# Strassen's seven products for gate and up in blocks 2 to 7, with weight sums kept in DRAM and streamed

## The chip, the cores and the metric

The kernel runs on one core of one Trainium2 chip. The metric is the device time of one execution in microseconds (us), as the median of several runs. Engines are named as in the profile: PE is TensorE's matmul, PEld its weight load, DVE is VectorE, ACT is ScalarE, POOL is GpSimd, SP is the engine that issues most DMAs.

## The reference, cut to what matters

Input x is 4 x 1024 tokens of 512 numbers in float32. Both branches start from one layer norm.

```python
xn = _layernorm(x)
# attention branch (16 heads of 32, chunks of 128 tokens, decaying state S per head)
h = _rmsnorm(xn, qkv_norm_w);  q, k, v = split(h @ _weight_quant(qkv_w).T)
scores = einsum('bhtd,bhsd,hts->bhts', q, k, mask)
o = scale * (scores @ v + (q * lam_t) @ S);  S = lam_T * S + (k * lam_rev).T @ v
attn = _rmsnorm(_rmsnorm(o, norm_w), proj_norm_w) @ _weight_quant(proj_w).T
# feed-forward branch, hidden width 2048
gate = xn @ w_gate.T;  up = xn @ w_up.T
ffn = (silu(gate) * up) @ w_down.T
return x + attn + ffn
```

## The kernel before

The 4096 tokens are cut into 8 blocks of 512. A block is 4 chunks of 128 tokens. Float32 operands are split into a high and a low float16 part, and a product is made of three matmuls (high x high, high x low, low x high); the quantized weights of the attention branch need one part, so theirs is made of two. `products` (line 517 is its matmul) issues them.

Each block is a list of items, and each engine has its own list, written out by hand: `FIRST_ORDER` for block 0, which also prepares the weights, and `STEADY_ORDER` for blocks 1 to 7. An engine runs its items strictly in that order and waits on semaphores that the other engines raise. The items are:

- `K`, `Q` (8 each, 256 tokens wide) and `V` (4, 512 columns): projections. ACT and DVE split the results (`K` and `Q` at L661 and L748), and SP copies them by DMA into `k_stack` and `q_stack` (three DMAs each, L935 and L937).
- `SC` (16): scores of four heads, L559. DVE multiplies by the mask (`SC`, L789), ACT and DVE split (`SC` at L673, `SL` at L747). `O` (L586, L588) and `OX` are the attention products, `KV` the update of the state.
- `G` and `U` for each of 16 tiles of 128 hidden columns: gate and up products, 12 matmuls of 512 columns each. ACT takes SiLU of the gate (L728), DVE multiplies by the up product (`U`, L908), ACT and DVE split the result (`UH` at L735, `UL` at L747).
- `D` (16): down products, 12 matmuls of 512 columns each, added to `y` by DVE (L861). `PJ` (4, 8 matmuls each): the output projection.
- `NA`, `NR`, `NZ`, `ZT`: the norms of the attention output and its transposes by DMA (L1019). `KT` is a transpose of K (L1015).
- `ST`, `XN`, `TX`, `TH`: statistics and norm of the next block's x, its split, and its transposes by DMA into `xt` (four of 1024 columns, L1007 and L1012) and `ht` (L999). The `xt` ones wait until all `G` and `U` of the block have run, since `xt` has one buffer. `YS` stores the output.

All gate and up weights stay in SBUF (`wg`, `wu`). PSUM has 8 banks: gate, up, scores, attention output, and four shared by the other products in turn.

## Time and profile before

| | |
|---|---|
| median of 3 runs | 1361.49 us (1361.11 to 1363.04) |
| the profiled execution's own time | 1361.45 us |
| its span | 1359.7 us |
| granted TensorE clock | 1.00 |
| PE busy | 1334.2 us (98%), 8332 matmuls |
| DVE busy | 924.6 us (68%) |
| ACT busy | 486.5 us (36%) |
| POOL busy | 67.5 us (5%) |
| DMA | 98.72 MB, mean 73 GB/s |

Busy times are unions of the instructions' spans. Spans of consecutive matmuls overlap, so the pace of a stream of matmuls is read from the starts of its first and next instructions, not from the mean duration. Block 1 runs from about 184.5 to 342.2 us and a steady block takes 164.6 us (671.7 to 836.3 is one).

### The profile page before, as it was taken

How to read it: one execution, taken by the hardware profiler on the slowest of the kernel's cores; microseconds unless marked ns; L12 is line 12 of the kernel's file. 1: busy time of each engine (PE TensorE's matmuls, PEld its weight loads, DVE VectorE, ACT ScalarE, POOL GpSimd, SP SyncE). 2: the span in 40 equal slices, each digit the busy share in tenths (PEclk: the TensorE clock that was granted, in tenths of full speed). 3: DMA queues.
4: the chain of work that ended last, by engine and by line, in shares of the span. 5: the costliest groups of instructions: out<-in, count | busy, mean ns of one | idle time of the engine just before them, and what ended most of it. 6: DMA issues, size and time to landing. Idle time of an engine off the chain costs nothing.

```text
span 1359.7 us, 21928 instructions
## 1 busy us (share of the span) xinstructions
PE 1334.2 (98%) x8332; PEld 721.3 (53%) x8332; DVE 924.6 (68%) x1886; ACT 486.5 (36%) x915; POOL 67.5 (5%) x88
## 2 busy tenths in 40 slices
PE   5899999999999999999999999999999999999999
PEld 3455555555455554555545555555545555455554
DVE  6988995576655766657766677657775576755655
ACT  7964633233233332333323233223332233232331
POOL 5600000000000000000000000000000000000000
DMA  8242234113431145211351113510145112431121
GB/s 314 83 142 67 87 73 120 26 32 67 111 88 28 30 79 124 53 32 40 71 140 35 29 40 70 148 40 26 38 85 132 32 30 49 94 94 32 32 48 47
DMA packets 193767, 98.72 MB, mean 73 GB/s; under 512 B 127104, under 2 KB 179328, under 8 KB 192000
## 3 DMA queue, kind: packets, MB, share of 16 engines
q1 hardware_dynamic: 193376, 97.30, 28.3%
q8 instruction: 68, 1.11, 0.4%
q14 instruction: 35, 0.29, 0.1%
q10 hardware_dynamic: 288, 0.01, 0.0%
HBM read 34.35 MB, written 8.39 MB: 31 GB/s over the span
## 4 chain that ended last, share of the span: by engine, by line
PE 94%; DVE 3%; ACT 1%; DMA 1%; SPq 1%; issue 1%; POOL 0%; DVEq 0%; POOLq 0%
PE bank L517 89%; PE bank L559 2%; PE bank L586 1%; PE bank L588 1%; DVE wg_lo L1292 0%; SPq L935 0%; DMA xin<-x 0%; ACT wg_lo L1142 0%; DMA k_stack<-k_parts 0%; DVE arena L861 0%; DMA q_stack<-q_parts 0%; DVE arena L747 0%; DVE xt L748 0%; DVE wd_lo L1292 0%; DVE wu_lo L1292 0%
## 5 line engine op out<-in xcount | busy, mean ns | idle before, releaser
L517 PE MATMUL bank<-wd_hi,arena 128*128 128x512 f16 x1024 | 317.0, 379 | 0.0
L517 PE MATMUL bank<-xt,wg_hi 128*128 128x512 f16 x1024 | 306.5, 381 | 3.6 <-ACT ql L728 1.6
L517 PE MATMUL bank<-xt,wu_hi 128*128 128x512 f16 x1024 | 304.6, 379 | 0.0
L517 PE MATMUL bank<-xt,wg_lo 128*128 128x512 f16 x512 | 195.0, 381 | 0.0
L517 PE MATMUL bank<-wd_lo,arena 128*128 128x512 f16 x512 | 194.0, 379 | 0.0
L517 PE MATMUL bank<-xt,wu_lo 128*128 128x512 f16 x512 | 194.0, 379 | 0.0
L517 PEld LDWEIGHTS bank<-wd_hi,arena 128*128 128x128 f16 x1024 | 100.2, 98 | 115.3
L789 DVE TENSOR_TENSOR sm<-bank,mask 128x512 f32<-128x512 f32 x128 | 88.1, 688 | 105.4 <-PE bank L559 105.3
L517 PEld LDWEIGHTS bank<-xt,wu_hi 128*128 128x128 f16 x1024 | 99.0, 98 | 104.4 <-issue 0.5
L517 PEld LDWEIGHTS bank<-xt,wg_hi 128*128 128x128 f16 x1024 | 98.2, 98 | 103.5 <-issue 4.6
L673 ACT ACTIVATE sm_hi<-sm 128x512 f16<-128x512 f32 x128 | 80.1, 626 | 193.5 <-DVE sm L789 193.5
L908 DVE SCALAR_TENSOR_TENSOR sg<-bank,small,sg 128x512 f32<-128x512 f32 x125 | 93.4, 747 | 76.7 <-ACT sg L728 41.4
L861 DVE SCALAR_TENSOR_TENSOR arena<-bank,small,arena 128x512 f32<-128x512 f32 x160 | 119.6, 748 | 36.0 <-PE bank L517 33.5
L728 ACT ACTIVATE sg<-bank,small 128x512 f32<-128x512 f32 x125 | 85.6, 685 | 130.1 <-PE bank L517 79.5
L517 PE MATMUL bank<-ht,wq 128*128 128x256 f16 x1024 | 124.8, 273 | 0.8 <-issue 0.8
L747 DVE TENSOR_TENSOR sm_lo<-sm,sm_hi 128x512 f16<-128x512 f32 x128 | 88.1, 688 | 52.4 <-ACT sm_hi L673 52.3
L517 PEld LDWEIGHTS bank<-ht,wq 128*128 128x128 f16 x1024 | 97.3, 98 | 14.6 <-issue 1.3
L747 DVE TENSOR_TENSOR arena<-sg,arena 128x512 f16<-128x512 f32 x125 | 85.6, 684 | 9.7 <-ACT arena L735 9.1
L735 ACT ACTIVATE arena<-sg 128x512 f16<-128x512 f32 x125 | 77.7, 622 | 34.6 <-DVE sg L908 34.4
L517 PEld LDWEIGHTS bank<-xt,wg_lo 128*128 128x128 f16 x512 | 50.2, 98 | 61.1 <-issue 1.1
L517 PEld LDWEIGHTS bank<-xt,wu_lo 128*128 128x128 f16 x512 | 50.0, 98 | 60.5
L661 ACT ACTIVATE k_parts<-bank 128x256 f16<-128x256 f32 x64 | 24.4, 382 | 155.5 <-PE bank L517 155.5
(200 smaller groups left out, 1492.2 us busy)
## 6 DMA issues: line engine op xcount, KB each, us to landing
k_stack<-k_parts SPq DMA_DIRECT2D x192, 64.0 KB, 2.2
q_stack<-q_parts SPq DMA_DIRECT2D x192, 64.0 KB, 2.2
arena<-x SPq DMA_DIRECT2D x8, 1024.0 KB, 5.9
out<-arena SPq DMA_DIRECT2D x32, 256.0 KB, 2.4
xin<-x SPq DMA_DIRECT2D x30, 256.0 KB, 4.5
stage<-up_t SPq DMA_DIRECT2D x4, 1024.0 KB, 5.3
stage<-down_t SPq DMA_DIRECT2D x4, 1024.0 KB, 4.9
stage<-gate_t SPq DMA_DIRECT2D x3, 1024.0 KB, 4.8
```

The source lines that it names most:

```text
L517: last = e.matmul(dst, a, b, start=start and n == 0, stop=stop and n == len(lhs) - 1)
L559: last = e.matmul(b_sc[:, P * h:P * (h + 1)], k_stack[:, h, t], q_stack[:, h, t], start=True, stop=True)
L586: e.matmul(both[:, h, :, :], smp[0][:, h, :], vh, start=h == 0, stop=False)
L588: last = e.matmul(both[:, h, 0, :], smp[1][:, h, :], vh[:, 0, :], start=False, stop=alone)
L661: e.activation(parts[:, 0, :], bank_of(it, blk)[:, 0:HALF], ACT.Copy, scale=QKV_SCALE).then_inc(ac[kind].sem, 1)
L673: e.activation(smp[0][:, :, :], sm[:, :, :], ACT.Copy).then_inc(ac["SM"].sem, 1)
L728: e.activation(gate_tile(blk, h), b_gate[:, :], ACT.Silu, scale=sgate[:, q:q + 1]).then_inc(ac["SILU"].sem, 1)
L735: e.activation(gated[q % 2][0][:, h % HPQ, :], gate_tile(blk, h), ACT.Copy).then_inc(ac["GH"].sem, 1)
L747: return e.tensor_tensor(dst, src, hi, ALU.subtract)
L789: e.tensor_tensor(sm[:, :, :], b_sc[:, :].rearrange("p (h t) -> p h t", h=HPG), mask[:, HPG * j:HPG * (j + 1), :], ALU.mult).then_inc(ve[" ...
L861: e.scalar_tensor_tensor(out=y[:, c, :], in0=bank_of(it, blk)[:, :], scalar=beta[:, 8:9] if kind == "PJ" else cd[:, it[1]:it[1] + 1], in1= ...
L908: e.scalar_tensor_tensor(out=gate_tile(blk, h), in0=b_up[:, :], scalar=cu[:, q:q + 1], in1=gate_tile(blk, h), op0=ALU.mult, op1=ALU.mult). ...
```

## The change

Blocks 0 and 1 keep the plain gate and up products (`PLAIN = 2`). Blocks 2 to 7 use the Winograd form of Strassen's scheme. For a tile, the gate and the up weights are the two rows of a 2 x 2 block matrix whose columns are the two halves of the 512 input features; x has the two halves of the features by two halves of the block's tokens. Seven products of such blocks take the place of eight. Each is a unit of six matmuls of 256 columns (2 slices of the contraction, 3 combinations of parts).

- **PE**: `G` and `U` give way to `TA` (two units), `TB` (three), `TC` (one), `TD` (one) for each tile.
- **ACT** copies partial sums out of PSUM at `TA`, `TB` and `TC` (s1, s2, s3, 256 columns each); its `TD` is SiLU on the finished gate tile. **DVE** adds them to other banks: `TA` (C11, 256 columns), `TC` (C2, 512), `TD` (C12, 256). **POOL** multiplies SiLU's result by the up tile (`UG`). `UH` and `UL` split that with the scale `cu`; `UL` becomes a scaled form.
- **x**: `TX` gives way to `XC`: POOL makes four sums of 256 columns per pair of chunks (`TT`), ACT and DVE split seven units of 256 columns, and SP transposes 3584 columns by one DMA, twice a block (`move_c`), into `xs`, which has one buffer.
- **Weights**: the sums of weights are made in block 1, one tile at a time in two slots: `BL` (two loads), `BS` (scale, ACT), `BA` (four sums, POOL), `BH` and `BC` (high and low parts of 1792 columns, ACT and DVE), `BX` (store of 128 x 3584 float16 to a DRAM tensor). From block 2 on `LW` on ACT's queue loads tile after tile into a ring of four buffers.
- Block 1 has an order of its own (`SECOND_ORDER`); `STEADY_ORDER` is written anew. The plain weights and the new buffers share one SBUF tensor, `wide`. Two shared banks are left in blocks 2 to 7. Scales by powers of two change (`X_SCALE` and others).

The diff, cut to its core:

```diff
--- before.py
+++ after.py
+UNITS = 7
+UNIT = KT * P // 2
+RING = 4
+PLAIN = 2
 SMALL = 267
...
-X_SCALE = 2.0 ** 10
+X_SCALE = 2.0 ** 9
 H_SCALE = 2.0 ** 9
+W_SCALE = 2.0 ** 12
+GATED_SCALE = 2.0 ** 5
...
+BUILD_SLOT = [0 if h < 2 else h % 2 for h in range(HT)]
...
 STEADY_ORDER = {
     "PE": [
-        ('K', 0), ('Q', 0), ('U', 0), ('V', 0), ('G', 0), ('V', 1), ('SC', 0, 0), ('G', 1), ('U', 1), ('KV', 0), ('O', 0, 0),
...
+        ('K', 0), ('V', 0), ('V', 1), ('Q', 0), ('TA', 0), ('TA', 1), ('TB', 0), ('TC', 0), ('TB', 1), ('TD', 0), ('TC', 1),
+        ('TA', 2), ('SC', 0, 0), ('TD', 1), ('TB', 2), ('TC', 2), ('O', 0, 0), ('SC', 0, 1), ('KV', 0), ('K', 1), ('TA', 3),
+        ('Q', 1), ('TD', 2), ('TB', 3), ('TC', 3), ('TA', 4), ('OX', 0, 0), ('O', 0, 1), ('SC', 1, 0), ('TD', 3),
...
+        ('D', 2, 3), ('D', 3, 0), ('D', 3, 1), ('PJ', 1), ('D', 3, 2), ('D', 3, 3), ('PJ', 2), ('PJ', 3),
...
-    wg = [sb(f"wg_{n}", [P, KT, HID], F16) for n in ("hi", "lo")]
-    wu = [sb(f"wu_{n}", [P, KT, HID], F16) for n in ("hi", "lo")]
+    wide = sb("wide", [P, NQ, 4 * KT * HID // NQ], F16)
...
+    b_work = [wide[:, n, 0:both].bitcast(F32) for n in range(2)]
+    b_out = [wide[:, n, both:2 * both] for n in range(2)]
+    f32_part = lambda start, n: wide[:, 0, 2 * start:2 * (start + n)].bitcast(F32)
+    gt = [f32_part(BLK * n, BLK) for n in range(3)]
+    up = [f32_part(BLK * (3 + n), BLK) for n in range(2)]
+    s1, s3 = (f32_part(5 * BLK + HALF * n, HALF) for n in range(2))
+    s2 = [f32_part(6 * BLK + HALF * n, HALF) for n in range(2)]
+    xs = wide[:, 1, 0:2 * both].rearrange("p (a t) -> p a t", t=HALF)
+    ring = [wide[:, 2 + n // 2, both * (n % 2):both * (n % 2 + 1)] for n in range(RING)]
+    comb = [wide[:, 2, 2 * both:2 * both + 2 * D].bitcast(F32), osq]
...
+        elif kind in ("TA", "TB", "TC", "TD"):
+            h = it[1]
+            one, two = b_tile[h % 2]
+            low, high = slice(0, HALF), slice(HALF, 2 * HALF)
+            def unit(dst, w, b, start=True):
+                for k in range(2):
+                    for n in range(3):
+                        last = e.matmul(dst, tile_weights(h, n // 2, w, k), tile_x(n % 2, b, k),
+                                        start=start and (k, n) == (0, 0), stop=(k, n) == (1, 2), skip_group_check=not start)
...
+            if kind == "TA":
...
+                e.wait_ge(ld_w[h % RING].sem, ld_w[h % RING].at(blk, 16 * (h // RING + 1)))
+                e.wait_ge(ve["C12"].sem, ve["C12"].at(blk, h - 1))
+                unit(one[:, low], 0, 0).then_inc(pe["P1"].sem, 1)
+                unit(two[:, low], 1, 1).then_inc(pe["P2"].sem, 1)
+            elif kind == "TB":
+                e.wait_ge(ac["S1"].sem, ac["S1"].at(blk, h + 1))
+                unit(one[:, low], 4, 4, start=False).then_inc(pe["P6"].sem, 1)
+                e.wait_ge(ve["C11"].sem, ve["C11"].at(blk, h + 1))
+                unit(two[:, low], 3, 6)
+                unit(two[:, high], 2, 3)
+            elif kind == "TC":
+                e.wait_ge(ac["S2"].sem, ac["S2"].at(blk, h + 1))
+                unit(one[:, low], 5, 5, start=False).then_inc(pe["P7"].sem, 1)
+            else:
+                e.wait_ge(ve["C2"].sem, ve["C2"].at(blk, h + 1))
+                unit(two[:, high], 6, 2, start=False).then_inc(pe["P3"].sem, 1)
         elif kind == "D":
             _, q, c = it
...
+        elif kind == "XC":
+            p = it[1]
...
+            dst = c_src[p]
+            e.wait_ge(moved_c[p].sem, moved_c[p].at(blk, 0))
+            e.activation(dst[:, 0:D], xin[:, 0, :], ACT.Copy).then_inc(ac["XC"].sem, 1)
+            e.activation(dst[:, D:D + UNIT], xin[:, 1, UNIT:D], ACT.Copy).then_inc(ac["XC"].sem, 1)
+            e.wait_ge(po["TT"].sem, po["TT"].at(blk, p + 1))
+            for n in range(2):
+                a = 3 * UNIT + D * n
+                e.activation(dst[:, a:a + D], comb[n], ACT.Copy).then_inc(ac["XC"].sem, 1)
+        elif kind == "TA":
+            h = it[1]
+            e.wait_ge(pe["P1"].sem, pe["P1"].at(blk, h + 1))
+            e.wait_ge(ve["C11"].sem, ve["C11"].at(blk, h))
+            e.activation(s1, b_tile[h % 2][0][:, 0:HALF], ACT.Copy).then_inc(ac["S1"].sem, 1)
+        elif kind == "TB":
+            h = it[1]
+            e.wait_ge(pe["P6"].sem, pe["P6"].at(blk, h + 1))
+            e.wait_ge(ve["C12"].sem, ve["C12"].at(blk, h - 1))
+            e.activation(s2[h % 2], b_tile[h % 2][0][:, 0:HALF], ACT.Copy).then_inc(ac["S2"].sem, 1)
+        elif kind == "TC":
+            h = it[1]
+            e.wait_ge(pe["P7"].sem, pe["P7"].at(blk, h + 1))
+            e.wait_ge(ve["C2"].sem, ve["C2"].at(blk, h))
+            e.activation(s3, b_tile[h % 2][0][:, 0:HALF], ACT.Copy).then_inc(ac["S3"].sem, 1)
+        elif kind == "TD":
+            h = it[1]
+            q, t = h // HPQ, gt[h % 3]
+            e.wait_ge(ve["C12"].sem, ve["C12"].at(blk, h + 1))
+            e.activation(t, t, ACT.Silu, scale=sgate[:, q:q + 1]).then_inc(ac["SILU"].sem, 1)
+        elif kind == "LW":
+            h = it[1]
+            if is_plain(blk):
+                e.wait_ge(st_b[BUILD_SLOT[h - HT]], 16 * turn(h - HT))
+                e.wait_ge(pe["U"].sem, pe["U"].at(blk, 12 if h < HT + 2 else HT))
+            else:
+                e.wait_ge(pe["P3"].sem, pe["P3"].at(blk, h - RING + 1))
+            e.dma_start(ring[h % RING], made[h % HT, :, :]).then_inc(ld_w[h % RING].sem, 16)
         elif kind == "G":
...
+        elif kind == "XC":
+            for n, (a, src) in enumerate(((0, xin[:, 0, :]), (D, xin[:, 1, UNIT:D]), (3 * UNIT, comb[0]), (5 * UNIT, comb[1]))):
+                size = UNIT if n == 1 else D
+                last = lo(dst[:, UNITS * UNIT + a:UNITS * UNIT + a + size], src, 1.0, dst[:, a:a + size], ac["XC"], 4 * p + n + 1)
+            last.then_inc(ve["XC"].sem, 1)
...
+        elif kind == "TA":
+            h = it[1]
+            e.wait_ge(ac["S1"].sem, ac["S1"].at(blk, h + 1))
+            e.wait_ge(pe["P2"].sem, pe["P2"].at(blk, h + 1))
+            e.wait_ge(po["GT"].sem, po["GT"].at(blk, max(h - 2, 0)))
+            e.tensor_tensor(gt[h % 3][:, 0:HALF], b_tile[h % 2][1][:, 0:HALF], s1, ALU.add).then_inc(ve["C11"].sem, 1)
+        elif kind == "TC":
+            h = it[1]
+            e.wait_ge(ac["S3"].sem, ac["S3"].at(blk, h + 1))
+            e.wait_ge(ve["GL"].sem, ve["GL"].at(blk, max(h - 1, 0)))
+            e.tensor_tensor(up[h % 2].rearrange("p (a t) -> p a t", a=2),
+                            b_tile[h % 2][1][:, :].rearrange("p (a t) -> p a t", a=2),
+                            s3.unsqueeze(1).to_broadcast([P, 2, HALF]), ALU.add).then_inc(ve["C2"].sem, 1)
+        elif kind == "TD":
+            h = it[1]
+            e.wait_ge(pe["P3"].sem, pe["P3"].at(blk, h + 1))
+            e.tensor_tensor(gt[h % 3][:, HALF:2 * HALF], b_tile[h % 2][1][:, HALF:2 * HALF], s2[h % 2], ALU.add)\
+                .then_inc(ve["C12"].sem, 1)
         elif kind == "U":
             h = it[1]
             q = h // HPQ
...
+        if it[0] == "UG":
+            h = it[1]
+            e.wait_ge(ac["SILU"].sem, ac["SILU"].at(blk, h + 1))
+            e.tensor_tensor(up[h % 2], up[h % 2], gt[h % 3], ALU.mult).then_inc(po["GT"].sem, 1)
+        elif it[0] == "TT":
+            p = it[1]
+            a, b, (t1, t2), (t3, t4) = xin[:, 0, :], xin[:, 1, :], *([t[:, 0:UNIT], t[:, UNIT:D]] for t in comb)
+            e.wait_ge(ve["XN"].sem, ve["XN"].at(blk, 2 * p + 2))
+            if is_plain(blk):
+                e.wait_ge(pe["U"].sem, pe["U"].at(blk, 3 * HPQ))
+            e.tensor_tensor(t3, b[:, UNIT:D], b[:, 0:UNIT], ALU.subtract).then_inc(po["T3"].sem, 1)
+            e.tensor_tensor(t1, b[:, 0:UNIT], a[:, 0:UNIT], ALU.subtract)
+            e.wait_ge(po["T3"].sem, po["T3"].at(blk, p + 1))
+            e.tensor_tensor(t2, t3, a[:, 0:UNIT], ALU.add).then_inc(po["T2"].sem, 1)
...
+                def move_c(p):
+                    if not is_plain(blk):
+                        e.wait_ge(pe["P3"].sem, pe["P3"].at(blk, HT))
+                    e.wait_ge(ve["XC"].sem, ve["XC"].at(blk, p + 1))
+                    e.dma_start_transpose(xs[:, :, P * p:P * (p + 1)], c_src[p]).then_inc(moved_c[p].sem, 16)
...
+                    elif kind == "BX":
+                        e.wait_ge(s_built, n + 1)
+                        e.dma_start(made[n, :, :], b_out[BUILD_SLOT[n]]).then_inc(st_b[BUILD_SLOT[n]], 16)
+                    elif kind == "BL":
+                        m, (q, i) = BUILD_SLOT[n], divmod(n, HPQ)
+                        e.wait_ge(pe["U"].sem, pe["U"].at(blk, HPQ * (m + 1)))
+                        if turn(n) > 1:
+                            e.wait_ge(s_built, max(g + 1 for g in range(n) if BUILD_SLOT[g] == m))
+                        for u, which in enumerate(("gate", "up")):
+                            e.dma_start(b_work[m][:, D * u:D * (u + 1)].rearrange("p (k c) -> p k c", k=KT),
+                                        dram[which][q, :, :, P * i:P * (i + 1)]).then_inc(ld_b[m], 16)
...
+                elif kind == "BA":
+                    a11, a12, s1_, a22, s2_, s3_, s4_ = (b_work[BUILD_SLOT[n]][:, UNIT * u:UNIT * (u + 1)] for u in range(UNITS))
+                    e.wait_ge(s_bscaled, n + 1)
+                    e.tensor_tensor(s3_, a11, s1_, ALU.subtract).then_inc(s_blink, 1)
+                    e.wait_ge(s_blink, 3 * n + 1)
+                    e.tensor_tensor(s1_, s1_, a22, ALU.add).then_inc(s_blink, 1)
+                    e.wait_ge(s_blink, 3 * n + 2)
+                    e.tensor_tensor(s2_, s1_, a11, ALU.subtract).then_inc(s_blink, 1)
+                    e.wait_ge(s_blink, 3 * n + 3)
...
+                elif kind == "BS":
+                    m = BUILD_SLOT[n]
+                    e.wait_ge(ld_b[m], 32 * turn(n))
+                    for u, which in enumerate(("gate", "up")):
+                        w, at = b_work[m][:, D * u:D * (u + 1)], PIECES.index((which, n // HPQ))
+                        last = e.activation(w, w, ACT.Copy, scale=ws[:, at:at + 1])
+                    last.then_inc(s_bscaled, 1)
+                elif kind == "BH":
+                    m = BUILD_SLOT[n]
+                    e.wait_ge(s_badd, n + 1)
+                    if turn(n) > 1:
+                        e.wait_ge(st_b[m], 16 * (turn(n) - 1))
...
+                elif kind == "BC":
+                    m = BUILD_SLOT[n]
+                    e.wait_ge(s_bhi, n + 1)
+                    e.tensor_tensor(b_out[m][:, UNITS * UNIT:both], b_work[m], b_out[m][:, 0:UNITS * UNIT], ALU.subtract)\
+                        .then_inc(s_built, 1)
...
```

## Rows read from the trace of the kernel before

**Rows 1.** The page: busy us, share of the span, instructions.

```profile
PE 1334.2 (98%) x8332; PEld 721.3 (53%) x8332; DVE 924.6 (68%) x1886; ACT 486.5 (36%) x915; POOL 67.5 (5%) x88
```

**Rows 2.** PE's waits: us in total, times, longest.

```profile
PE bank L1168 <- ACT wg_lo L1142: 12.6, 2, 12.1
PE bank L517 <- ACT ql L728: 1.6, 1, 1.6
```

**Rows 3.** Windows: length; PE, PEld, DVE, ACT, POOL busy; clock, DMA share, GB/s.

```profile
671.70:836.30 164.60, 164.60 (x1034) 88.46 (x1032) 109.33 (x222) 52.03 (x104) 3.81 (x4) 1.00 0.27 65
...
184.50:342.20 157.70, 156.37 (x985) 85.06 (x984) 104.81 (x213) 50.65 (x102) 3.91 (x4) 1.00 0.29 67
```

**Rows 4.** PE's timeline: start us, us, instruction.

```profile
707.85 0.60 PE L517 MATMUL bank<-xt,wg_hi 128*128 128x512 f16 x2
...
710.44 0.59 PE L517 MATMUL bank<-xt,wu_hi 128*128 128x512 f16 x2
...
713.80 1.91 PE L517 MATMUL bank<-ht,wq 128*128 128x256 f16 x16
715.55 0.59 PE L517 MATMUL bank<-xt,wg_hi 128*128 128x512 f16 x2
```

**Rows 5.** Groups by form: busy us, mean ns | idle before.

```profile
L908 DVE SCALAR_TENSOR_TENSOR sg<-bank,small,sg 128x512 f32<-128x512 f32 x125 | 93.4, 747 | 76.7 <-ACT sg L728 41.4 <-PE bank L517 35.0
...
L728 ACT ACTIVATE sg<-bank,small 128x512 f32<-128x512 f32 x125 | 85.6, 685 | 130.1 <-PE bank L517 79.5 <-DVE arena L747 50.6
L747 DVE TENSOR_TENSOR arena<-sg,arena 128x512 f16<-128x512 f32 x125 | 85.6, 684 | 9.7 <-ACT arena L735 9.1
...
L822 DVE TENSOR_TENSOR arena<-bank,arena 128x256 f32<-128x256 f32 x64 | 27.1, 423 | 45.5 <-ACT arena L686 45.1
...
L686 ACT ACTIVATE arena<-bank 128x256 f32<-128x256 f32 x64 | 24.5, 382 | 66.2 <-PE bank L517 66.2
...
L1292 DVE SCALAR_TENSOR_TENSOR wd_lo<-stage,small,wd_hi 128x1024 f16<-128x1024 f32 x8 | 9.9, 1278 | 0.0
...
L1136 ACT ACTIVATE wd_hi<-stage,small 128x1024 f16<-128x1024 f32 x8 | 8.9, 1146 | 0.0
```

**Rows 6.** Timeline of POOL, then of DVE, block 0.

```profile
44.05 1.98 POOL L1084 TENSOR_SCALAR wu_lo<-wu_lo,small 128x1024 f32<-128x1024 f32 x1
46.12 1.04 POOL L1085 TENSOR_SCALAR wu_lo<-wu_lo 128x1024 f32<-128x1024 f32 x1
...
57.85 0.62 POOL L1090 TENSOR_SCALAR lam_q<-lam_q 128x512 f32<-128x512 f32 x1
...
44.96 0.68 DVE L747 TENSOR_TENSOR ht<-bank,ht 128x512 f16<-128x512 f32 x1
...
46.22 2.02 DVE L1292 SCALAR_TENSOR_TENSOR wu_lo<-stage,small,wu_hi 128x1024 f16<-128x1024 f32 x1
```

**Rows 7.** DMA issues: count, KB each, median us to landing.

```profile
q_stack<-q_parts SPq DMA_DIRECT2D x192, 64.0 KB, 2.2
...
out<-arena SPq DMA_DIRECT2D x32, 256.0 KB, 2.4
...
stage<-gate_t SPq DMA_DIRECT2D x3, 1024.0 KB, 4.8
...
xt<-stage SPq DMA_TRANSPOSE x28, 3.1
```

**Rows 8.** Timeline of SP, then of PE, around step 1.

```profile
718.49 0.60 SPq L937 DMA_DIRECT2D q_stack<-q_parts  x1
...
720.95 0.38 PE L559 MATMUL bank<-q_stack,k_stack 96*128 96x128 f16 x4
```

**Rows 9.** Timeline at a block's end: PE, SP, PE.

```profile
671.68 0.19 PE L586 MATMUL bank<-v,sm_hi 128*128 128x64 f16 x1
...
687.55 3.44 SPq L1012 DMA_TRANSPOSE xt<-stage  x2
...
698.99 0.59 PE L517 MATMUL bank<-xt,wu_hi 128*128 128x512 f16 x2
```

294 lines of the change are left out of this document (203 added, 91 removed), and 152 rows, old and new, of tables (SECOND_ORDER, STEADY_ORDER, ve).

## The prediction

> **What bounds the kernel now.** The page's busy table comes first: TensorE (PE) is busy for 1334.2 us, 98% of the span [rows 1]. A busy share alone does not say who waits, so the list of PE's waits comes next. Its largest entry is 12.6 us in the opening, and the next is 1.6 us [rows 2]. Then the windows: in one steady block, 671.7 to 836.3 us, PE is busy for all 164.60 us, DVE for 109.33, ACT for 52.03, the DMA share is 0.27, and the granted clock is 1.00. Block 1 (184.5 to 342.2) shows 156.37 of 157.70 [rows 3]. So PE's stream of matmuls sets the end, and whatever leaves that stream is a gain, as long as nobody new makes PE wait. Every engine runs a hand-written order in sequence, so one late result stops all that stands behind it.
>
> **The matmuls removed (blocks 2 to 7).** The timeline gives the pace, since durations overlap. A gate product G is 12 matmuls of 512 columns, from 707.85 to 710.44 us: 2.59 us, 216 ns each. A K and a Q product are 16 matmuls of 256 columns, from 713.80 to 715.55: 1.75 us, 109.4 ns each [rows 4]. A tile's G and U cost 24 x 216 ns = 5.18 us. The new tile is 7 units x 6 = 42 matmuls of 256 columns, 42 x 109.4 = 4.59 us. The weight loads double in rate, but K and Q already run at one load per 256 columns, so 109.4 ns holds it. Saved: 0.585 us x 16 tiles x 6 blocks = 56 us. Blocks 0 and 1 issue the same matmuls as before. This is also the most the change can give: 1361.45 - 56 = 1305.
>
> **Work added to ACT and DVE (steady).** From [rows 5]: DVE loses U (0.75) and gets TA 0.42, TC 0.69 (512 columns) and TD 0.42 per tile; UL goes from 0.68 to the scaled form, 0.75. That is +0.85 us x 16 = 14 us. XC computes 2 x 1792 columns of low parts where TX computed 4 x 512, +2 us. DVE comes to 109 + 16 = 125 of a block of 164.6 - 9.4 = 155.2 us: 81%. ACT gets three copies of 256 columns, 3 x 0.38 x 16 = 18 us, some 2 us in XC and 20 DMA issues, about 80 of 155. Neither is a bound on its sum. Hidden under PE they cost nothing; if one stood on the path, its excess would be paid in full. Inside a tile the waits are short and covered: TB's first unit waits for a copy (0.38) made while the other tile's TA (1.3 us) runs, TC's result (S3, then C2: 0.38 + 0.69) has TA or TB of the next tile (1.3 to 2.0 us) before TD needs it. SiLU's product moves to POOL (UG), and UL stands behind it in DVE's order. Two shared banks instead of four: a product waits until the one before last is emptied. At the tightest place, V(1) behind K(0), that takes 0.38 + 2 x 0.42 us under V(0)'s 8 x 216 ns = 1.73 us; 0.5 us of slack, charged at nothing. The changed powers of two cost no instruction.
>
> **POOL beside DVE.** No row shows a two-input product of 512 columns on POOL. Nearest rows: one input of 512 columns took 0.62 us; one input of 1024, which reads as much as two of 512, took 1.04 at 46.12 and 1.98 at 44.05 [rows 6]. I take 1.1 us inside 0.62 to 2.0. What contention does is in the same group. DVE's 1024-column operation at 46.22 reads two SBUF operands and took 2.02 us, just behind POOL's start at 46.12 (its usual mean is 1.28 [rows 5]). The one at 44.96 reads PSUM and took 0.68 us beside POOL, no more than elsewhere. In a steady block DVE will have 88 instructions with two SBUF operands (16 SL, 16 UL, 16 state sums, 8 KT, 8 head products, 8 in XC, four each of NA, NZ, ZT and H), some 50 us. POOL will be busy 16 x 1.1 + 8 x 0.6 = 22 us of 155, 14%. 88 x 0.14 x half of 1.1 = 7 us more on DVE, 132 in all, 85%. Still under PE, so I charge nothing. The lower bound of this term is 0; the upper, each of the 88 waiting 0.55 us, is 48 us, and DVE would then take 173 us a block, above the old PE time.
> The Trainium skill (SBUF — State Buffer, on the shared port pair) says that a DVE instruction with two SBUF inputs and a GpSimd instruction that reads SBUF exclude each other, the later fully blocked. The slowed and the undisturbed row above agree with it, and it speaks against this change. By the rule at its worst the sum would be rival D's; by the rows' overlap it stays as it is.
>
> **The weight stream.** Each tile's sums are 128 x 3584 f16, 0.9 MB, 16 of them a block. A 1024 KB load lands after 4.8 us and a 256 KB transfer after 2.4 [rows 7], so 768 KB cost 2.4 us and a tile 2.8: 45 us a block, over the 44 us of 0.27 x 164.6. With 3072 more columns to transpose (4 us, priced below) the share is about 0.6, no bound. The ring of four keeps loads some three tiles (25 us) ahead. The price is delay for the small copies. The last copy of Q(1) into its stack is issued at 718.49 us and takes 2.2 us [rows 7]; the score product runs at 720.95 [rows 8]: 0.25 us of slack. The new order leaves 4.9 us between Q(1) and SC(1,0), and sends K 1.3 us earlier, so SP is free: 0.6 (ACT) + 1.3 (issue) + 2.2 = 4.1, 0.6 to 0.8 us of slack. A step meets a weight load with chance 45/155 = 0.3 and is held 1.4 us on average. 8 steps x 0.3 x (1.4 - 0.6) = 1.9 us a block, 11 us in all (0 if the loads always fall between; 8 x 1.4 x 6 = 67 if they always collide).
>
> **The block's end (steady).** Before, the last attention product starts at 671.68, the last x transpose is the second of the two issued in the 3.44 us from 687.55, so issued about 689.8 and landed 3.1 us later, 692.9, and U(0) reads it at 698.99 [rows 7, 9]: slack 6 us on a chain of 21. After, the chain gets POOL's four sums (4 x 0.6 = 2.4 us), 0.5 us of longer copies, and a transpose of 3584 columns in place of 1024. Of the 3.1 us for 1024 columns the part that grows with size is between 0.9 (a 64 KB copy's 2.2 us taken off) and 3.1; I take 1.4, near the lower end, so 2560 columns more are 3.5 us (2.3 to 7.8). ZT moved behind XN gives back 1.3. Chain: 26.1 us. Cover from O(7,1) to TA(0), with V(0) and V(1) now ahead: TD .66, six D 15.5, three PJ 5.2, K, V, V, Q 5.2 = 26.6. Slack 0.5 us, and the load LW 18 issued just before it takes up to 2.8 us of the same queues. I charge 1 us x 5 = 5 (0 to 4 each, so up to 20).
>
> **Block 1, where the sums are made.** 16 times: two loads, BS (2 x 0.69), four POOL sums (2.6), BH (1792 columns, from 1.15 for 1024: 1.7), BC (from 1.28 and 0.68: 2.2), a store [rows 5]. With the load, 3 to 5 us, a slot turns in 10.8 to 12.9 us before any queueing. From D(0,0) to D(2,3) PE has 16 G and U, 11 D and small work, 81 us, for six turns: 13.5 us each. DVE is at 105 + 34 = 139 of 158. Nearly no room for three in-order queues, and POOL's 64 sums meet DVE's. I charge 8 us, between 0 and 3 us x 7 turns + 4 = 25. What is late then is BX(15), st_b, both transposes and TA(0) of block 2.
>
> **Sum.** 1361.45 (this execution's time; the median of the runs is 1361.49) - 56 + 11 + 5 + 8 = 1329.5, say 1330.
>
> **Rivals.**
> A. Everything is hidden: 1305 to 1315. For: before, PE waited for nothing in steady blocks although a chain had 0.25 us of slack. Against: DVE goes from 66% to 85%. Chance 0.2.
> B. The forecast, 1315 to 1345: chance 0.55.
> C. The block's end and block 1 cost their upper bounds, 20 and 25 us, with 11 us inside the blocks: 1361.45 - 56 + 56 would be no gain at all, and part of that gives 1345 to 1358. For: the 0.5 us of slack; a store and two long transposes behind the last sum. Chance 0.13.
> D. The other side: POOL and DVE exclude each other at nearly each of the 88 instructions. PE waits at all once DVE's blocked time passes 155 - 125 = 30 us a block, and the gain is gone at 39.4 us; at 48 us the block takes 173 us, 6 x 8.4 = 50 us slower, 1412. For: the rows at 44 to 47 us. Against: POOL's 22 us leave little to block. Chance 0.07.
> E. C in full, or C with part of D, so that nothing or less than nothing is left, 1358 to 1370: chance 0.05.
>
> Faster by more than 0.2% (2.7 us, about what a measurement of this kernel can tell from no change): A, B and C, 0.88; within it 0.03 and slower 0.09, from D and E. The range from 1307 to 1352 holds most of A, all of B and two thirds of C, 0.81.
>
> **What would show it.** In the windows of a steady block: length 157 to 160 us, PE idle 2 to 5 us. 256-column matmuls at 109 ns, 42 a tile; if they pace at 115 or more, the 56 us is wrong. In PE's waits: rows released by stack copies, by xs transposes at each TA(0), and in block 1 by the sums. DVE busy near 130 us, POOL's product near 1.1 us; if POOL shows 2 us or PE waits mostly for DVE's C2 and C12, D was at work. A block 1 longer than 185 us would make the time longer than the range allows.

## The result and the profile after

The changed kernel takes 1538.93 us (median of four runs, 1534.20 to 1550.50); the kernel before took 1362.26 beside it (1361.11 to 1364.17). The ratio is 1.131, with a 95% interval of 1.124 to 1.138: 13% slower, where 1330 us was forecast. The profiled execution took 1534.20 us, its span is 1532.4.

From the page after: busy time, then PE's granted clock and the DMA share in 40 slices (compare [rows 1]).

```profile
PE 1339.8 (87%) x10060; PEld 903.7 (59%) x10060; DVE 1088.7 (71%) x2118; ACT 648.5 (42%) x1275; POOL 294.3 (19%) x296
...
PEclk9999999999889999999999999899998999989999
DMA  7232342477955349553594435944468543595342
```

PE's busy time is about what it was, but it is now 87% of the span: PE is idle for 193 us where it was idle for 25. PE's waits name the places (as in [rows 2]). Columns: us in total, times, longest. L811 is the first unit of a Strassen tile, L721 the score product.

```profile
PE bank L811 <- issue: 38.1, 6, 9.2
PE bank L721 <- issue: 34.3, 10, 6.2
PE bank L721 <- DMA k_stack<-k_parts: 25.6, 20, 3.3
PE bank L721 <- DMA q_stack<-q_parts: 22.1, 8, 4.0
PE bank L679 <- DVE arena L1109: 21.7, 17, 4.4
```

82 us stand ahead of score products, which wait for their stacked operands; 38 stand ahead of the first tile of a block, six times, once in each block that follows the building or a Strassen block. Windows of block 1 and of the first two Strassen blocks (columns as in [rows 3]), cut at SP's issue of the load of x into y, which comes once a block:

```profile
212.30:422.90 210.60, 178.69 (x1047) 92.88 (x1048) 151.79 (x241) 99.83 (x157) 72.49 (x76) 0.94 0.64 181
422.90:613.40 190.50, 167.05 (x1339) 120.69 (x1337) 131.24 (x258) 71.87 (x157) 30.91 (x28) 0.96 0.57 137
613.40:799.40 186.00, 165.37 (x1333) 120.31 (x1331) 129.55 (x255) 71.98 (x158) 30.72 (x28) 0.96 0.58 141
```

DVE's 131 us and the DMA share of 0.57 are as forecast (132 and 0.6). What is new is the length, 186 to 190 us against 155 us of matmuls, and a clock of 0.96. Cut at the same issue, the blocks of the kernel before are 164 to 166 us long, block 1 among them.

One such wait from near, in block 2: four lines of SP and ACT (what they issue), then three of PE.

```profile
438.12 1.25 SPq L1234 DMA_DIRECT2D q_stack<-q_parts  x2
439.41 0.60 SPq L1236 DMA_DIRECT2D q_stack<-q_parts  x1
...
438.37 0.33 ACTq L966 DMA_DIRECT2D wide<-made  x1
...
440.99 0.33 ACTq L966 DMA_DIRECT2D wide<-made  x1
```

```profile
448.05 0.59 PE L721 MATMUL bank<-q_stack,k_stack 96*128 96x128 f16 x4 [6.24 <-issue]
448.43 1.48 PE L811 MATMUL bank<-wide 128*128 128x256 f16 x6
449.71 0.63 PE L679 MATMUL bank<-state,ql 128*128 128x128 f32 x2
```

ACT issues two weight loads, one 0.25 us after SP's first copy and one 1.6 us after its last. The last copy is issued at 439.41, and a copy usually takes 2.2 us; PE starts only at 448.05, 8.6 us later, after 6.24 us of idleness. The view of q_stack has 8.6 us as its longest landing, so this is the copy that PE waited for, though the profile shows the wait as "issue". The windows over this stretch show what follows (granted clock and DMA share are the two numbers before the last):

```profile
440.00:444.00 4.00, 1.81 (x23) 1.55 (x21) 1.33 (x3) 0.81 (x3) 1.27 (x1) 1.00 1.46 285
444.00:448.00 4.00, 0.00 (x0) 0.00 (x0) 0.00 (x0) 0.00 (x0) 0.00 (x0) 0.82 0.51 166
448.00:452.00 4.00, 3.95 (x21) 3.04 (x22) 1.02 (x2) 0.72 (x3) 0.00 (x0) 0.50 0.20 61
```

PE stood still from 441.8 to 448.0 and then worked at a granted clock of 0.50, the lower of its two levels (1.2 of 2.4 GHz): six matmuls of 256 columns take 1.28 us from start to start (448.43 to 449.71), 213 ns each, against 109 at the full clock. So a wait is paid a second time. In "PE busy" this shows as work, which is why PE is as busy as before with 56 us less of it to do.

The block's end. SP's two long transposes of the sums of x, at the end of block 1, and PE's first tile of block 2:

```profile
392.41 4.21 SPq L1288 DMA_TRANSPOSE wide<-stage  x1
399.35 13.01 SPq L1288 DMA_TRANSPOSE wide<-xt  x1
```

```profile
416.67 1.65 PE L811 MATMUL bank<-wide 128*128 128x256 f16 x7 [8.11 <-issue]
```

The DMA issues (count, KB, median us to landing; transposes without KB) and, below them, the last line of the view of k_stack:

```profile
wide<-made ACTq DMA_DIRECT2D x96, 896.0 KB, 5.6
...
out<-arena SPq DMA_DIRECT2D x32, 256.0 KB, 10.4
```

```profile
wide<-stage SPq DMA_TRANSPOSE x6, 6.4
wide<-xt SPq DMA_TRANSPOSE x6, 17.0
...
DMA to landing us min/median/max: 2.1/2.2/9.4
```

A copy still lands after 2.2 us in the median; only some are late, by up to 7 us. Copies are not alone in this: the transposes into `stage`, K's among them, land after up to 11.9 us (9.1 before). The second transpose takes 17 us in the median, the first, of the same size, 6.4.

### The profile page after: what moved, and what is told of

The parts are those of the page before. It is cut to its first block, busy times and chain, and to the rows that moved or that the text cites. A ratio compares the mean times of both kernels' runs of the same rounds, so it can differ in the third digit from the quotient of the medians.

```text
span 1532.4 us, 26734 instructions
## 1 busy us (share of the span) xinstructions
PE 1339.8 (87%) x10060; PEld 903.7 (59%) x10060; DVE 1088.7 (71%) x2118; ACT 648.5 (42%) x1275; POOL 294.3 (19%) x296
## 4 chain that ended last, share of the span: by engine, by line
PE 55%; DVE 18%; issue 9%; DMA 8%; SPq 5%; ACT 3%; POOL 2%; ACTq 0%; DVEq 0%; POOLq 0%
PE bank L679 30%; PE bank L811 22%; DMA k_stack<-k_parts 4%; SPq L1234 3%; DVE stage L995 2%; DMA q_stack<-q_parts 2%; PE bank L721 2%; DVE arena L1109 2%; DVE wide L1661 1%; DMA wide<-up_t 1%; SPq L1335 1%; DVE sm_lo L995 1%; DVE xin L1132 1%; DVE sm L1037 1%; SPq L1236 1%
## 5 line engine op out<-in xcount | busy, mean ns | idle before, releaser
L811 PE MATMUL bank<-wide 128*128 128x256 f16 x4032 | 498.2, 281 | 38.3 <-issue 38.1
L811 PEld LDWEIGHTS bank<-wide 128*128 128x128 f16 x4032 | 402.8, 101 | 100.6 <-issue 40.9
L1204 POOL TENSOR_TENSOR wide<-wide 128x512 f32<-128x512 f32 x96 | 125.9, 1314 | 823.8 <-ACT wide L958 823.8
L679 PE MATMUL bank<-xt,wide 128*128 128x512 f16 x768 | 178.1, 387 | 6.7 <-ACT sg L972 3.3
L679 PEld LDWEIGHTS bank<-xt,wide 128*128 128x128 f16 x768 | 75.1, 100 | 94.7 <-issue 9.9
L721 PE MATMUL bank<-q_stack,k_stack 96*128 96x128 f16 x512 | 50.9, 223 | 82.1 <-issue 34.3
L1174 DVE TENSOR_TENSOR wide<-bank,wide 128x512 f32<-128x512 f32 x96 | 66.1, 689 | 50.4 <-ACT wide L953 48.8
L1169 DVE TENSOR_TENSOR wide<-bank,wide 128x256 f32<-128x256 f32 x96 | 40.2, 419 | 63.9 <-ACT wide L943 47.7
L1180 DVE TENSOR_TENSOR wide<-bank,wide 128x256 f32<-128x256 f32 x96 | 40.3, 419 | 63.5 <-PE bank L811 62.7
L721 PEld LDWEIGHTS bank<-q_stack,k_stack 96*128 96x128 f16 x512 | 31.9, 98 | 88.7 <-issue 88.3
L679 PEld LDWEIGHTS bank<-wd_lo,arena 128*128 128x128 f16 x512 | 50.8, 99 | 52.4 <-issue 3.1
L996 DVE SCALAR_TENSOR_TENSOR arena<-wide,small,arena 128x512 f16<-128x512 f32 x96 | 80.6, 840 | 0.4
```

The lines of the kernel that those rows point to most:

```text
L679: last = e.matmul(dst, a, b, start=start and n == 0, stop=stop and n == len(lhs) - 1)
L721: last = e.matmul(b_sc[:, P * h:P * (h + 1)], k_stack[:, h, t], q_stack[:, h, t], start=True, stop=True)
L811: last = e.matmul(dst, tile_weights(h, n // 2, w, k), tile_x(n % 2, b, k), start=start and (k, n) == (0, 0), stop=(k, n) == (1, 2), skip_g ...
L996: return e.scalar_tensor_tensor(out=dst, in0=src, scalar=scale, in1=hi, op0=ALU.mult, op1=ALU.subtract)
L1174: e.tensor_tensor(up[h % 2].rearrange("p (a t) -> p a t", a=2), b_tile[h % 2][1][:, :].rearrange("p (a t) -> p a t", a=2), s3.unsqueeze(1) ...
L1180: e.tensor_tensor(gt[h % 3][:, HALF:2 * HALF], b_tile[h % 2][1][:, HALF:2 * HALF], s2[h % 2], ALU.add)\
```

## The experiments

Unless said otherwise each ran once, beside the kernel before, which took 1361.3 to 1363.7 us (the median where it ran several times). The changed kernel's own runs differ by 16 us from each other, so smaller steps from it are not read. The kernel with all loads issued by SP took 1401.6 us in one series and 1407.2 to 1409.3 in another; from it, steps under 8 us are not read. Lengths of blocks 1 to 6, cut as above:

| kernel | us | block 1 | blocks 2 to 6 |
|---|---|---|---|
| before | 1361.5 | 164.3 | 164.3, 165.8, 163.6, 165.5, 164.1 |
| changed | 1534.2 | 210.5 | 190.6, 186.0, 187.0, 183.4, 196.8 |
| small loads | 1393.5 | 209.6 | 165.3, 162.8, 161.2, 162.8, 165.5 |
| small transposes | 1483.0 | 207.7 | 179.7, 178.5, 177.6, 174.4, 181.8 |
| loads from SP (timed run) | 1408.7 | 205.9 | 169.4, 168.3, 165.5, 164.1, 170.3 |
| the same, small vectors and transposes | 1374.2 | 206.2 | 163.3, 161.1, 159.3, 157.9, 162.2 |
| the same, small building | 1392.6 | 190.0 | 168.7, 168.2, 165.9, 164.7, 169.7 |
| before, with a stream from ACT | 1410.6 | 164.4 | 169.6, 177.3, 171.2, 177.4, 170.9 |

### Which part of the change costs it

**Small weight loads.**

```diff
-            e.dma_start(ring[h % RING], made[h % HT, :, :]).then_inc(ld_w[h % RING].sem, 16)
+            n = both if is_plain(blk) else 64
+            e.dma_start(ring[h % RING][:, 0:n], made[h % HT, :, 0:n]).then_inc(ld_w[h % RING].sem, 16)
```

> From block 2 on each weight load moves 64 of the 3584 columns (16 KB instead of 896 KB); the first four tiles are still loaded whole, all waits stay. The products of the later tiles are made with stale weights. Theory W (the weight stream delays the small stack copies and the transposes, PE stands still for them and then runs at half clock): PE's waits for the score products fall from 82 us in all to under 15, the slowest stack copy lands in under 5 us instead of 9.4, and the time falls by 90 to 150 us, to 1385 to 1445. Rival P (DVE and POOL exclude each other): the waits remain, the time falls by less than 30 us. Rival T (the long transposes at the block's end by themselves): the waits at the first tile of each block, 38 us, remain.

Measured: 1393.49 us, 141 less than the profiled execution of the changed kernel. PE's waits:

```profile
PE bank L679 <- DVE arena L1110: 22.8, 17, 4.7
...
PE bank L721 <- DMA k_stack<-k_parts: 12.0, 13, 1.8
PE bank L811 <- issue: 9.2, 1, 9.2
...
PE bank L721 <- DMA q_stack<-q_parts: 5.5, 2, 3.3
PE bank L721 <- issue: 4.0, 6, 1.6
```

The waits at score products go from 82 to 21.5 us, those at a block's first tile from six to one (block 2's, behind block 1), the mean clock from 0.959 to 0.987. Of the 141 us, 104 are PE's idle time (193 to 89) and 37 its busy time (1339.8 to 1302.9), the same matmuls at a higher clock. The time is inside what theory W expected; the waits at score products, 21 of them even without the stream, stay above its 15 us. The stream is most of the loss, and the kernel without it is still slower than before.

**Small POOL product** (rival D).

```diff
-            e.tensor_tensor(up[h % 2], up[h % 2], gt[h % 3], ALU.mult).then_inc(po["GT"].sem, 1)
+            e.tensor_tensor(up[h % 2][:, 0:8], up[h % 2][:, 0:8], gt[h % 3][:, 0:8], ALU.mult).then_inc(po["GT"].sem, 1)
```

> POOL's product of SiLU and up is made on 8 of 512 columns; the rest of the up tile passes on unmultiplied. All waits stay. Theory W: DVE's two-operand instructions return to their durations of before (0.68 us instead of 0.71 to 0.84), but PE's waits for copies stay and the time falls by less than 25 us. Rival P: DVE's results come earlier everywhere and the time falls by 80 us or more.

Measured: 1522.16 us, less than the runs of the changed kernel differ. DVE is busy for 122 to 124 us of a block in place of 129 to 131, and the waits at score products stay (89 us). D is not what made it slow by 13%.

**Small x transposes** (1024 of 3584 columns, as many as the kernel before moved at once).

```diff
-                    e.dma_start_transpose(xs[:, :, P * p:P * (p + 1)], c_src[p]).then_inc(moved_c[p].sem, 16)
+                    n = 28 if is_plain(blk) else 8
+                    e.dma_start_transpose(xs[:, 0:n, P * p:P * (p + 1)], c_src[p][:, 0:n * P]).then_inc(moved_c[p].sem, 16)
```

> From block 2 on the transposes of the x combinations move 1024 of 3584 columns, twice a block; the other columns keep block 1's values, so later blocks multiply stale x. Rival T, that these transposes are the main loss: the waits at each block's first tile, 38 us, go, with their share of the half clock, and the time falls by 60 us or more. Theory W: those waits shrink only in part, because the weight loads queue beside them, and the score product's 82 us stay; the time falls by 20 to 50 us.

Measured: 1483.04 us, 51 less. The first tile waits once for 7.9 us instead of six times for 38; the score products still wait for 86. So the long transposes cost some 50 us, 30 of it PE's waits at the first tile, but only inside the stream: with small loads the same transposes, whole, made no first tile wait from block 3 on.

**Loads and stores in pieces of 1 KB** in place of 7 KB for each partition; the whole function is computed. The edit keeps the sums in DRAM as seven units.

```diff
-    made = nc.dram_tensor("made", (HT, P, both), F16).ap()
+    made = nc.dram_tensor("made", (HT, UNITS, P, both // UNITS), F16).ap()
```

> The whole function; the weight sums lie in DRAM in pieces of 1024 bytes instead of 7168 a partition, same bytes, same number of DMAs. If the DMA engines take turns between the queues descriptor by descriptor (W1), a small copy waits for 1 KB pieces instead of 7 KB pieces: the slowest stack copy lands in 3 to 5 us instead of 9.4 and the time falls by 40 to 120 us. If what counts is the bytes in flight (W2), the landings stay at 8 us and the time stays within 15 us of 1534, or grows because more descriptors are issued on ACT's queue.

Measured: 1490.35 us. The second transpose lands after 10.3 us in place of 17.0, and the first tile waits once for 3.6 us in place of six times for 38. But the copies' worst stay at 9.2 and the score products' waits at 79. The time falls as W1 expected and the copies do as W2 expected: smaller pieces help the transposes, not the copies.

### The moment and the queue of the loads

**All weight loads of blocks 2 to 7 issued by SP**, one to two behind a step's copies and its K transpose; the whole function is computed.

```diff
-        ... ('LW', 5) to ('LW', 19) in ACT's order
+        ('KT', 0), ('LW', 4), ('LW', 5), ... ('KT', 1), ('LW', 6), ('LW', 7), ... in SP's order
+                    elif kind == "LW" and not is_plain(blk):
+                        scalar_item(e, it, blk)
```

> The whole function; from block 2 on the weight loads are issued by SP, one or two behind each step's stack copies and K transpose, instead of by ACT whenever its order comes to them. Theory W with the moment of issue as the cause: every small copy is ahead of the loads in the same queue, PE's waits for the score products fall from 82 us to under 25, the 17 us of the second x transpose fall to 7, and the time falls to 1395 to 1430. Rival: what counts is the total of bytes in a block, whoever issues them; then the waits stay above 60 us and the time above 1490. Rival: SP, which now stands on TD before it issues the loads, becomes late with the copies; then the waits for score products grow.

Measured: 1401.61 us. SP's timeline in block 2 shows the order: copies, transpose, loads, and the next copies 7.5 us after the loads. Below it the last line of the view of k_stack.

```profile
431.56 1.25 SPq L1234 DMA_DIRECT2D q_stack<-q_parts  x2
432.85 0.61 SPq L1236 DMA_DIRECT2D q_stack<-q_parts  x1
433.68 1.21 SPq L1337 DMA_TRANSPOSE stage<-stage  x1
434.94 1.57 SPq L966 DMA_DIRECT2D wide<-made  x2
442.41 1.22 SPq L1234 DMA_DIRECT2D k_stack<-k_parts  x2
```

```profile
DMA to landing us min/median/max: 2.1/2.2/3.5
```

The worst landing is 3.5 us in place of 9.4, the second transpose 6.1 in place of 17.0, with the same bytes at the same share (0.56). PE's waits at score products go from 82 to 21 us. So the bytes alone don't do it; what is in flight when a small transfer is issued does. Being in one queue doesn't spare a transfer: the stores of the output, which SP issues right behind two loads, land here after 7.6 us in the median, against 2.7 with small loads.

**The same with 1 KB pieces:** 

> The same with the weight sums in pieces of 1024 bytes in DRAM. If the order in the queue has already taken away the meeting of copies and loads, pieces add nothing: within 8 us of the run with the loads on SP. If loads still overtake or hold copies, pieces give another 10 to 40 us, as they gave 44 alone.

Measured: 1407.59 us; nothing more is gained.

**The loads issued by SP, timed:** 

> The same kernel as the one with all weight loads issued by SP behind each step's copies, timed: 1400 to 1404 us, ratio to the kernel before 1.027 to 1.032, so still slower.

Measured: 1408.00 us (1407.19 to 1409.25), ratio to the kernel before 1.033, interval 1.031 to 1.035. This is the best that computes the whole function, and it is slower than before, also by 4 us more than the 1404 expected.

**The stream alone, in the kernel before.** 96 loads of 896 KB, issued by ACT in front of each SiLU of blocks 2 to 7, into the low half of the down weights; the down products read the high half in its place.

```diff
+    def stream(e, blk, h):
+        n, k = h % 2, (HT * (blk - 2) + h) // 2
...
+        e.dma_start(spare[n], down_t[h // HPQ, :, :, :].rearrange("p i n -> p (i n)")[:, 0:1792]).then_inc(ld_spare[n], 16)
...
         kind = it[0]
+        if kind == "G" and blk >= 2:
+            stream(e, blk, it[1])
```

> The kernel before, with the stream of 896 KB loads added in blocks 2 to 7: 16 a block, each issued by ACT in front of gate tile h's SiLU, into what was the low half of the down weights; the down products read the high half in its place, so the output differs from the reference's and the matmuls and their count stay. Theory W (large loads in flight hold back the 64 KB stack copies, whatever the kernel): the copies' longest landing goes from 4.0 us to 8 or more, PE waits at the score products, the clock falls after some of these waits, and the time goes from 1362 to 1430 to 1500 us. Rival N (it is the new order, its long transposes and its later vectors that have no slack; the old order bears the stream): 1362 to 1375 us.

Measured: 1410.61 us, 48 more than the kernel before beside it (1362.5): clear of rival N, but less than the 1430 to 1500 that theory W expected, as is the longest landing (8 us expected). The first two of PE's waits (L569 is the score product; of L527's 13.6 us, 12.9 are two waits at the product behind K's transpose), and k_stack's landings:

```profile
PE bank L569 <- issue: 20.4, 12, 2.7
PE bank L527 <- issue: 13.6, 3, 6.7
...
DMA to landing us min/median/max: 2.1/2.2/6.2
```

**The same loads issued by SP**, two behind each K transpose: 

> As the run with the stream issued by ACT, but SP issues the same 96 loads, two behind each step's K transpose. W: the copies of the next step come 15 us later, when the loads have landed; copies stay under 5 us and the time is 1362 to 1380 us. If bandwidth and not the moment of issue is what counts, it is as slow as the run with ACT's loads.

Measured: 1363.87 us, 1.4 more than before, within the noise. So it is not the bytes. Queue and moment of issue changed together here, as in the kernel with SP's loads; the stores above speak for the moment, but loads issued by ACT at SP's moments were not tried.

**ACT's loads in pairs**, in front of every second SiLU:

```diff
-        if kind == "G" and blk >= 2:
+        if kind == "G" and blk >= 2 and it[1] % 2 == 0:
             stream(e, blk, it[1])
+            stream(e, blk, it[1] + 1)
```

> The kernel before with ACT's stream again, the same 96 loads of 896 KB, now two at once in front of every second SiLU (as before, the down products read the high half in place of the low one). If copies wait behind all that the other queue has in flight, the worst landing goes from 6.2 to 9 us or more and the time from 1410.6 to 1440 to 1480 us. If only the share of time with a load in flight counts, both stay: 6 us, 1405 to 1415.

Measured: 1435.50 us, 73 more than before; k_stack's and q_stack's worst landings are 8.0 and 8.5 us. The time is a little below the 1440 us and more that was expected, the longest landing a little below the 9. Single loads, issued at least 3.8 us apart, held a copy for up to 4.0 us beyond its usual 2.2, and pairs for up to 6.3 (the longest landing without loads, 4.0 us, is 1.8 beyond); a load itself took 5.1 us in the median, in pairs 6.3. So at worst a copy is held for about as long as what is in flight takes, and not for a mean part of it. The Trainium skill (DMA: Bandwidth & Descriptors, on queues, rings and completion order) says that each DMA engine takes turns between the queues that have work, and drains a whole packet of one before it switches. The longer hold behind pairs agrees with more packets ahead, but no run shows how much of a load is one packet; how much of the hold is sharing and how much is waiting in turn stays open. ACT's order in the change has such pairs, LW 8 and 9, 10 and 11, 13 and 14, 16 and 17.

### Block 1

**Small stores of the sums** (64 of 3584 columns from the third on; the loads read the first two tiles' sums in place of all): 

> Block 1 stores 64 of 3584 columns of each tile's sums from the third tile on, and all later loads read the first two tiles' sums. Block 1 took 210.6 us against 164.3. If its loss is DMA traffic of the stores (W in block 1), it falls by 20 us or more; if it is the work of making the sums on the three engines' orders (rival B), by less than 8 us.

Measured: 1546.27 us, block 1 203.9 in place of 210.5: 7 less, so the stores' traffic is at most a small part of the loss.

**Small sums** (the four engines' work on 8 columns): 

> Block 1 scales, adds and splits 8 columns where it had 256 to 1792; loads, stores and waits stay, and the sums are wrong. Rival B (the orders of DVE, ACT and POOL have no room for 45 to 72 us of making sums, and PE waits for what stands behind it): block 1 falls by 25 us or more. Theory W in block 1: it falls by less than 15 us.

Measured: 1530.71 us, block 1 190.4: 20 less, between the two expectations. In both runs the total is inside the changed kernel's spread, so only block 1 is read.

**Small sums, stores and reads, with the weight loads issued by SP:**

```diff
-    a11, a12, s1_, a22, s2_, s3_, s4_ = (b_work[BUILD_SLOT[n]][:, UNIT * u:UNIT * (u + 1)] for u in range(UNITS))
+    a11, a12, s1_, a22, s2_, s3_, s4_ = (b_work[BUILD_SLOT[n]][:, UNIT * u:UNIT * u + 8] for u in range(UNITS))
... and so BS, BH, BC; the store of 64 columns, the reads of 16 of 128
```

> The changed kernel with weight loads issued by SP, and block 1's building made small: sums on 8 columns, stores of 64 columns, reads of 16 of 128 columns (leaves out the sums themselves). Block 1 took 205.4 us in the kernel with SP's loads, 158 in the kernel before. If the building's work on the engines and queues is what lengthens it, block 1 takes 160 to 175 us and the time is 1362 to 1375. If its place in the orders is (each engine waits for the next in a chain of small steps), block 1 stays above 185.

Measured: 1392.60 us, block 1 190.0 in place of 205.9 in the timed kernel beside it. That is above 185, the mark of the second explanation. (The 158 us of the expectation is block 1 in another cut; in this one it took 164.3.) Of the 41.6 us over those 164.3, 16 are the building's work and 26 are there without it. Block 1 of the kernel before and of this run:

```profile
210.47:374.77 164.30, 162.97 (x1020) 87.83 (x1019) 107.68 (x218) 51.75 (x104) 3.92 (x4) 1.00 0.28 65
213.50:403.50 190.00, 173.88 (x1056) 93.69 (x1057) 113.91 (x241) 62.57 (x158) 28.51 (x76) 0.96 0.44 96
```

PE is idle for 16.1 us where it was for 1.3, and busy for 10.9 us more at a lower clock, which makes the 26. The idle time lies at four places: two score products (3.54 and 1.84 us) and these two.

```profile
382.29 1.89 PE L679 MATMUL bank<-ht,wq 128*128 128x256 f16 x8 [5.18 <-DVE arena L1109]
397.30 6.96 PE L811 MATMUL bank<-wide 128*128 128x256 f16 x45 [7.07 <-issue]
```

These two stand at the new order's turn from plain to Strassen blocks: the one behind DVE's adds, the other at the first tile of block 2, which needs both transposes behind the last store.

### What the Strassen blocks lose without the stream's delays

**POOL's product on 8 columns, loads from SP:** 

> The changed kernel with the weight loads issued by SP (1401.6 us) and POOL's product of gate and up on 8 of its 512 columns (leaves out most of that product). Theory P (what is left of PE's idle time in a steady block, some 8 us, comes from DVE being held by POOL): DVE's busy time falls from 130 to 123 us a block and blocks from 167 to 160 us, time 1365 to 1375. Rival B (two shared banks, whose adds on DVE come late because of DVE's order, not its speed): 1398 to 1403 us, DVE a few us less busy.

Measured: 1393.72 us, blocks 167.6, 165.5, 161.8, 163.4, 165.9: 1 to 4 us less each, and 8 to 16 us less in all, between the two expectations.

**DVE's adds TA, TC and TD on 8 columns, loads from SP:** 

> The changed kernel with the weight loads issued by SP, and DVE's three adds of each tile (TA, TC, TD) on 8 columns in place of 256, 512 and 256 (leaves out most of the tile's recombination). It takes some 20 us of work from DVE in each block. If DVE's load is what makes PE wait for the adds into y and for the head products, the blocks go from 167 to about 160 us and the time to 1365 to 1375. If it is the number of shared banks or the transfers, 1395 to 1402.

Measured: 1402.82 us, no change that can be read. PE's waits for adds and head products in blocks 2 to 6 do fall, from 18 to 11 us, and block 1 is 4 us longer than in the same kernel with whole adds, 209.6 for 205.4.

**Both, and x transposes of 1024 columns, loads from SP:** 

> The changed kernel with weight loads issued by SP, and in blocks 2 to 7 both POOL's product and DVE's three adds of a tile on 8 columns, and the x transposes of 1024 of 3584 columns (leaves out most of the recombination and of the inputs' sums). All matmuls stay. If what the steady blocks lose (162 to 169 us against 155 of matmuls) is lost to the added vectors and transposes, they take 156 to 159 us here, 1340 to 1360 in all. If the two shared banks and the order lose it, 161 or more.

Measured: 1374.24 us, 34 less than the same kernel with whole vectors in the same series, all of it in blocks 2 to 6 (803.8 against 837.6 us). At 158 to 163 us they lie between the two expectations, 3 to 8 us longer than their 155 us of matmuls.

**Three late operations one place earlier on DVE, loads from SP.** The whole function is computed.

```diff
-        ... ('SC', 7, 1), ('TH', 0), ('KV', 7), ... ('TH', 1), ('D', 2, 0), ... ('ST', 1), ('D', 2, 3), ...
+        ... ('SC', 7, 1), ('KV', 7), ('TH', 0), ... ('D', 2, 0), ('TH', 1), ... ('D', 2, 3), ('ST', 1), ...
```

The reason was this stretch of the kernel with SP's loads: PE's wait, then DVE around it.

```profile
716.52 0.39 PE L679 MATMUL bank<-wd_hi,arena 128*128 128x512 f16 x1 [0.99 <-DVE arena L1109]
```

```profile
713.66 0.68 DVE L1174 TENSOR_TENSOR wide<-bank,wide 128x512 f32<-128x512 f32 x1
714.26 1.53 DVE L995 TENSOR_TENSOR wide<-xin,wide 128x512 f16<-128x512 f32 x1
715.72 0.74 DVE L1109 SCALAR_TENSOR_TENSOR arena<-bank,small,arena 128x512 f32<-128x512 f32 x1
```

DVE is never idle here: the add that frees PE's bank stands behind a low part of 1.53 us, in place of the usual 0.68. Beside it POOL makes its product:

```profile
713.98 1.27 POOL L1204 TENSOR_TENSOR wide<-wide 128x512 f32<-128x512 f32 x1 [8.06 <-ACT wide L958]
```

The low part reads two operands in SBUF. It begins 0.28 us after POOL's product, which ends at 715.25, and is 0.85 us longer than usual; with POOL's product on 8 columns the low part at this place takes 0.68 us, and the wait is gone. So this wait is rival D's mechanism at one place, where DVE has no slack.

> The changed kernel with weight loads issued by SP, and in DVE's order of blocks 2 to 7 three late operations one place earlier: the head product KV(7) ahead of TH(0), the add of D(2,0) ahead of TH(1), the add of D(2,3) ahead of the statistics ST(1). The whole function is computed. If their place in the order makes PE wait, each of the three waits of 0.6 to 1.0 us in a block goes and the time falls by 6 to 15 us. If PE then waits for what was pushed back, no change within 3 us.

Measured: 1414.84 us, no gain, and 6 us more than the slowest of the same kernel's runs, more than the 3 that the rival allowed. Of the three waits (0.63, 0.99 and 0.93 us in block 3) one of 0.46 is left, and the next one has grown from 0.73 to 2.34:

```profile
734.93 1.25 PE L659 MATMUL bank<-wp,stage 128*128 128x512 f16 x5 [2.34 <-DVE arena L1089]
```

PE's waits in blocks 2 to 6, summed by what they stand at, us, and the five blocks' length (776 us would be the forecast's pace, 823.3 less 5 x 9.4):

| kernel | product behind K's transpose | DVE's adds and head products | score products | length |
|---|---|---|---|---|
| small loads | 0 | 19 | 11 | 817.6 |
| loads from SP (timed run) | 12 | 18 | 10 | 837.6 |
| the same, small POOL product | 10 | 7 | 10 | 824.3 |
| the same, small adds | 11 | 11 | 12 | 830.7 |
| the same, both and small transposes | 2 | 6 | 10 | 803.8 |
| the same, three operations earlier | 10 | 15 | 14 | 842.9 |

Making POOL's product small takes the most off the waits for DVE. The waits of the first column come with whole loads (11 us in the changed kernel too): in block 3 of the single run one of 3.40 us ends 5.9 us after SP began to issue two loads behind K's transpose. They nearly go when the x transposes are small too, so what PE's idle time loses in that run is half transfers and half vectors.

## Why the prediction was wrong

**Where the 229 us between 1305 and 1534 lie.** Small loads take off 141. Of the other 88, block 1 has 209.6 - 164.3 = 45; blocks 2 to 6 have 817.6 - (823.3 - 5 x 9.4) = 41; 2 are left for blocks 0 and 7.

**The step that failed: the weight stream, 11 us, upper bound 67; measured 141.** Three things in it were wrong.
1. The delay of one copy. I took the mean rest of one load, 1.4 us, less the slack of 0.6 to 0.8. A copy is in fact held for up to 4.0 us with single loads and 6.3 with pairs, and ACT's order has pairs. The waits at score products grew by 60 us.
2. The long transposes. I priced each at 6.6 us at the block's end, beside one load (2.8 us); in the stream the second took 17 us. This is the term "block's end", 5 us with an upper bound of 20, and it is some 50. It exists only with the stream, so it is part of the 141. (Alone the second took 6.4 us: that price was right.)
3. The clock. No term had it. After 6 us of waiting PE worked at half its clock for some microseconds, and 37 of the 141 us are this. A sum of waits is too small by it: on 104 us of idleness 37 came on top.
The average that I called "no bound", a DMA share of 0.6, was right (0.57) and said nothing of this: the kernel with the same share and SP's loads is 130 us faster.

**Block 1, 8 us, upper bound 25; measured 45.** I counted only how fast a slot turns. The building's work is 16 of it. 26 stay when the work is made small, from four waits and a lower clock, two of the waits at the turn into block 2, the place that I named ("what is late then") but gave 4 us. The other 3 are not placed; the same block took 204.7 to 209.6 us in kernels that do the same in it. POOL's four sums took 3.7 us a tile where I took 2.6.

**The steady blocks, DVE at 85% "hidden under PE", 0 us; measured 41 in blocks 2 to 6 without the stream, 8 a block.** PE's waits are 30 of the 41: 19 for DVE's adds and head products, most of them at the block's end, where DVE has no idle moment, and 11 at score products. The other 11 are in PE's busy time, and no run says by what. The waits for DVE come in part from POOL's product: with it small they are 7 in place of 18 in the kernel with SP's loads. A busy share over the block, 80%, says nothing of its end. The slack of 0.5 us that I charged at nothing, V(1) behind K(0), held: no wait stands before a V product. Whether two shared banks in place of four cost anything is not shown: more than two can't be had beside the tiles' four, and moving the adds only moved the wait.

**What was right.** The matmuls' pace at full clock: below, 48 of 256 columns take 5.24 us from start to start, 109 ns each (kernel with SP's loads). With small vectors and transposes a block comes down to 157.9 us. DVE's busy time, 129 to 131 us for 132. Rival D stayed small in busy time: POOL's product took 1.31 us (I took 1.1), DVE's scaled low part 0.84 for 0.75, and the scores' low part 0.71 for 0.69.

```profile
695.95 5.40 PE L811 MATMUL bank<-wide 128*128 128x256 f16 x48
701.19 0.39 PE L679 MATMUL bank<-state,ql 128*128 128x128 f32 x2
```

```profile
L1204 POOL TENSOR_TENSOR wide<-wide 128x512 f32<-128x512 f32 x96 | 125.9, 1314 | 823.8 <-ACT wide L958 823.8
...
L995 DVE TENSOR_TENSOR sm_lo<-sm,sm_hi 128x512 f16<-128x512 f32 x128 | 90.9, 710 | 22.6 <-ACT sm_hi L872 22.2
...
L996 DVE SCALAR_TENSOR_TENSOR arena<-wide,small,arena 128x512 f16<-128x512 f32 x96 | 80.6, 840 | 0.4
```

The Trainium skill (SBUF — State Buffer, on the shared port pair) says that a DVE instruction with two SBUF inputs and a GpSimd instruction that reads SBUF exclude each other. The rows agree: the low part at 714.26 was held beside POOL's product, and DVE has 7 us less to do in a block when the product is small. But that is a seventh of rival D's 48. None of the rivals was what happened in the main: the slower ones were put on POOL and DVE or bounded at no gain, and a stream that holds back copies stood inside the forecast, with a bound that a mean had made.

## What to carry to other kernels

A stream of large loads is not priced by its share of the DMA engines' time but by the slack of each small transfer that can be issued while a load is in flight: bound it by the whole of what is in flight, at each place with little slack, and add the clock that PE loses after a wait. Issue such loads from the queue that issues the urgent copies, right behind them: the same 96 loads cost the kernel before 48 us from another queue at other moments and 1.4 us so. Before a change is built on a stream, add the stream alone to the kernel at hand and run that.

A kernel in which PE never waits has no slack that the profile shows; even without the stream, 8 of the 9 us that a block gained in PE's work were lost again, most of them in waits under 2 us, on DVE's adds at the block's end and on copies. Look there for DVE's work with two SBUF operands beside POOL's.

## What the runs showed of the hardware

- A 64 KB copy lands after 2.2 us. With single 896 KB loads of another queue, issued 3.8 us apart or more, the longest took 6.2 us; with pairs 8.5, and 9.4 in the changed kernel. With the same loads issued by SP behind the copies it took 4.1 (3.9 to 4.0 without loads).
- A transpose of 3584 columns took 6.2 and 6.4 us in the medians (the first and the second of a block) without the stream, and 6.4 and 17.0 with it; with loads in pieces of 1 KB the second took 10.3. The piece size did nothing for the plain copies.
- A DVE subtraction of 512 columns with two SBUF operands took 1.53 us beside a POOL product (1.27 us, begun 0.28 earlier) and 0.68 us when that product was small.
- After 6.2 us without a matmul PE's granted clock was 0.50 for the next 4 us and 0.83 for the 4 after them. The mean over the changed kernel was 0.959, and 0.987 without the stream; in blocks 2 to 6 with SP's loads, with waits of up to 3.9 us, it was 0.99 to 1.00.
